# Attention with 32 groups of four heads: side work between the steps, tiles by twos, another engine for the maxima

## What is computed

```python
qkv = (x @ Wqkv + bqkv).reshape(B, L, 3, n_heads, head_dim)
scores = jnp.einsum('bqhd,bkhd->bhqk', q, k) / math.sqrt(head_dim)
scores = scores + slopes[None, :, None, None] * bias[None, None]
probs = jax.nn.softmax(scores, axis=-1)
out = jnp.einsum('bhqk,bkhd->bqhd', probs, v).reshape(B, L, D)
return out @ Wout + bout
```

## Time and profile before

| | us |
|---|---|
| median of three runs | 3262.87 |
| lowest, highest | 3258.28, 3268.13 |
| the profiled execution: its own time | 3271.27 |
| its span, first to last instruction | 3269.5 |
| attention, first to last exponential | 1250.1 to 2919.5 |
| PE busy over the span | 3085.7 (94%) |
| DVE, ACT, POOL busy | 2534.6, 1985.8, 1094.2 |
| mean granted TensorE clock | 0.952 of full speed |

### The profile page before, as it was taken

How to read it: one execution, slowest core, us unless ns; L and a number is a source line. 1 busy time by engine, 2 the same in 40 slices (tenths; PEclk the granted TensorE clock), 3 DMA queues, 4 the chain that set the end, 5 groups by cost and what they waited for, 6 DMA issues and landing times. The chain is left out here.

```text
span 3269.5 us, 73440 instructions
## 1 busy us (share of the span) xinstructions
PE 3085.7 (94%) x28196; PEld 1827.7 (56%) x28196; DVE 2534.6 (78%) x5875; ACT 1985.8 (61%) x2967; POOL 1094.2 (33%) x1364
## 2 busy tenths in 40 slices
PE   7999999995999869999999999999999999988999
PEld 3666666664788734444454444444544445437888
DVE  6677877764788658888888889788888887927887
ACT  2455444441666515777777777767777777775665
POOL 3354554443223221332423333323233232222222
PEclk8899999985999958999999999999999999998999
DMA  1000000002111151324232323232322322202111
GB/s 54 2 28 28 28 28 28 20 10 73 66 59 59 39 108 36 58 39 83 40 67 55 57 63 60 43 77 52 71 48 49 74 49 53 57 18 93 52 60 38
DMA packets 126461, 165.34 MB, mean 51 GB/s; under 512 B 23584, under 2 KB 104240, under 8 KB 125456
## 3 DMA queue, kind: packets, MB, share of 16 engines
q1 hardware_dynamic: 115688, 149.37, 18.7%
q0 software_dynamic: 9984, 10.38, 2.4%
q10 hardware_dynamic: 440, 0.90, 0.1%
HBM read 81.58 MB, written 38.24 MB: 37 GB/s over the span
## 5 line engine op out<-in xcount | busy, mean ns | idle before, releaser
L1855 ACT ACTIVATE b_p_t<-banks 128x1024 f32<-128x1024 f32 x1024 | 1040.2, 1027 | 304.0 <-PE banks L1742 238.7
L1681 PE MATMUL banks<-b_k_stack,b_q_stack 62*128 62x512 f32 x2048 | 809.6, 475 | 26.5 <-issue 10.8
L1742 PE MATMUL banks<-b_q_stack,b_k_stack 64*128 64x512 f32 x2048 | 767.8, 450 | 9.9 <-ACT b_p_t L1855 9.9
L1941 DVE CUSTOM_DVE_ANT_1 banks<-banks,b_near_rows 128x512 f32<-128x512 f32 x960 | 649.0, 715 | 138.3 <-PE banks L1681 135.1
L1944 DVE TENSOR_REDUCE b_half_max<-banks 128x1 f32<-128x512 f32 x1024 | 657.8, 684 | 79.9 <-PE banks L1681 76.3
L1696 PE MATMUL banks<-b_p_t,b_v 128*17 128x256 f32 x8192 | 631.8, 386 | 6.3 <-POOL b_p_t L2100 5.5
L1742 PEld LDWEIGHTS banks<-b_q_stack,b_k_stack 64*128 64x128 f32 x2048 | 313.7, 185 | 389.1 <-issue 325.5
L2100 POOL TENSOR_TENSOR b_p_t<-b_p_t,b_fall 128x256 f32<-128x256 f32 x384 | 280.5, 733 | 658.6 <-ACT b_p_t L1855 657.8
L1681 PEld LDWEIGHTS banks<-b_k_stack,b_q_stack 62*128 62x128 f32 x2048 | 341.9, 188 | 111.6 <-DVE b_half_max L1941 35.9
L1696 PEld LDWEIGHTS banks<-b_p_t,b_v 128*17 128x17 f32 x8192 | 142.8, 95 | 300.7 <-issue 162.2
L1148 ACT ACTIVATE ffn_relu<-banks,ffn_scale_fc 128x512 f32<-128x512 f32 x256 | 176.2, 688 | 205.5 <-PE banks L1080 205.5
(11 more groups left out here) (255 smaller groups left out, 5333.6 us busy)
## 6 DMA issues: line engine op xcount, KB each, us to landing
ffn_x<-x SPq DMA_DIRECT2D x32, 512.0 KB, 3.9
b_q_stack<-b_qk_hi SPq DMA_DIRECT2D x252, 64.0 KB
b_k_stack<-b_qk_hi SPq DMA_DIRECT2D x252, 64.0 KB
b_fall<-c_fall SPq DMA_DIRECT2D x48, 256.0 KB, 2.6
a_x<-hidden_states SPq DMA_DIRECT2D x16, 512.0 KB, 3.9
x<-a_x SPq DMA_DIRECT2D x16, 512.0 KB, 2.9
x<-ffn_x SPq DMA_DIRECT2D x16, 512.0 KB, 2.8
b_x<-x SPq DMA_DIRECT2D x8, 1024.0 KB, 5.6
```

Of the source, the lines that this page charges most:

```text
L1681: pe.matmul(m, q_stack[rows, slot, qb * P:(qb + 1) * P], k_stack[rows, slot, half * BANK:(half + 1) * BANK], start=True, stop=True, tile_p ...
L1742: last = pe.matmul(out, k_stack[stack, slot, kb * P:(kb + 1) * P], q_stack[stack, slot, half * BANK:(half + 1) * BANK], start=True, stop=n ...
L1855: act.activation(p_t[use % P_BUFS][:, :, :], scores[use % 2], ACT.Exp, scale=slopes()[pair][0]).then_inc(p_made, 1)
L1941: dve.tensor_tensor_reduce(out=m, in0=m, in1=near_window(pair, qb, rg), scale=1.0, scalar=LOWEST, op0=ALU.add, op1=ALU.max, accum_out=larg ...
```

## The change

- `attend` gives way once for each use instead of once for each score product (all five engines), and counts 32 steps: side work stands between uses.
- `make_stacks` counts 12 steps; the two projections are its steps 1 and 3, which fall ahead of use 4 and ahead of use 9. ACT evacuates each projection once (`qk`); POOL makes `qk_hi` from it by a copy and then `qk_lo`.
- SP issues the four transfers of bias rows (`stack_bias`) at step 1, before it waits for `qk_lo`; the 24 others follow the second projection as before, in the order of heads 0, 2, 1, 3, which is the order in which the maxima need them.
- Values and output tiles are made two at a time: twelve matmuls into one bank, one copy of 512 columns, one addition of 512 columns. `att_hi`, `att_lo` and `y` are now one buffer each of double width where there were two. Within a step of the output PE makes the product of the earlier two tiles before the transposes of the next two, and ACT copies in the same order.
- The maxima are transposed after the fourth of the next group's maxima (`turn == TURN - 1`, TURN is 4), and DVE copies the result out, ahead of its fifth maximum, instead of ACT. POOL's part, and SP's, stand at turn 5 instead of turn 3, one use later.

```diff
@@ schedule
-        STEPS, STACKS, VALUES, NORMALIZE = GROUP * HALVES * QB, 2, QB, 1 + QB
-        LEAD, TURN = 16, 2
+        STEPS, STACKS, VALUES, NORMALIZE = GROUP * HALVES * QB, 12, QB // 2, 1 + QB
+        STACK_STEPS = {1: 0, 3: 1}
+        LEAD, TURN = 16, 4
...
-                side_by_side(*([(STEPS, attend(g, rows), 1)] if g >= 0 else []),
+                side_by_side(*([(STEPS // ROWGROUPS, attend(g, rows), 1)] if g >= 0 else []),
...
-                             *([(STACKS, stacks(g + 2), 3)] if 0 <= g + 2 < ALL else []),
+                             *([(STACKS, stacks(g + 2), 1)] if 0 <= g + 2 < ALL else []),
...
+        IN_TURN = [pair + rg * PAIRS for pair in range(PAIRS) for rg in range(ROWGROUPS)]
@@ attend, on every engine
                     if rg == ROWGROUPS - 1:
                         follow(t, pair)
-                    yield
+                        yield
@@ tensor, find_maxima
-                    if g and turn == TURN:
-                        m, (used, n) = misc.take(("turn", g - 1), (shift_copied, g))
-                        pe.wait_ge(used, n)
-                        pe.wait_ge(row_max_made, g)
...
                         yield
+                    if g and turn == TURN - 1:
+                        m, (used, n) = misc.take(("turn", g - 1), (shift_copied, g))
+                        pe.wait_ge(used, n)
+                        pe.wait_ge(row_max_made, g)
...
+                    if g < ALL:
                         yield
@@ tensor, conclude
+                for n in range(TWOS + 1):
+                    tiles = TWOS * b + n
+                    if n:
+                        m, (used, value) = misc.take(("y", b, n - 1), (y_made, tiles))
+                        pe.wait_ge(used, value)
+                        pe.wait_ge(att_lo_made, tiles)
...
+                        last.then_inc(y_ready, 1)
+                    if n < TWOS:
+                        m, (used, value) = misc.take(("att", b, n), (att_lo_made, tiles + 1))
+                        pe.wait_ge(used, value)
...
                         last.then_inc(att_turned, 1)
@@ scalar, make_stacks
-                    act.activation(qk_hi[:, cols], m, ACT.Identity, bias=b_scaled[:, hg:hg + 1],
-                                   scale=scale_qk[:, 0:1]).then_inc(qk_hi_made, 1)
@@ scalar, find_maxima
-                        act.activation(shift_full[:, :], m, ACT.Copy, scale=-1.0).then_inc(shift_copied, 1)
@@ vector, find_maxima
+                    if g and turn == TURN:
+                        dve.wait_ge(max_turned, g)
+                        if g >= 2:
+                            dve.wait_ge(shift_made, g - 1)
+                        dve.tensor_scalar(shift_full[:, :], misc.at["turn", g - 1][0:2 * GROUP * QB, 0:P], -1.0, None, ALU.mult).then_inc(shift_copied, 1)
@@ gpsimd, make_stacks
-                    pool.wait_ge(qk_hi_made, use + 1)
...
+                        pool.tensor_copy(qk_hi[:, cols], qk[:, cols]).then_inc(qk_hi_made, 1)
+                        pool.wait_ge(qk_hi_made, use + 1)
+                        pool.tensor_tensor(qk_lo[:, cols], qk[:, cols], qk_hi[:, cols].bitcast(F32), ALU.subtract).then_inc(qk_lo_made, 1)
@@ sync, make_stacks
                 yield
-                yield
                 sp.wait_ge(bias_cast, 16)
+                if g >= SETS:
+                    sp.wait_ge(col_scores, STEPS * (g - SETS + 1))
+                for i in IN_TURN:
+                    stack_bias(sp, g, i)
+                for _ in range(max(STACK_STEPS) - 1):
+                    yield
                 sp.wait_ge(qk_hi_made, 2 * (g + 1))
                 sp.wait_ge(qk_lo_made, 2 * (g + 1))
-                if g >= SETS:
-                    sp.wait_ge(col_scores, STEPS * (g - SETS + 1))
-                for i in range(GROUP):
+                for i in IN_TURN:
                     if g or i < PAIRS:
                         stack_head(sp, g, i)
```

210 lines of the change are left out of this document (105 added, 105 removed).

## The result

The kernel after takes **3226.8 us** (median of 6 runs) where the kernel before, run beside it, takes 3260.6 (6 runs): a ratio of **0.9911, 95% interval 0.9883 to 0.9940**, some 29 us less (the two medians differ by 34). The profiled execution has 3227.1 us, its span is 3225.3, its mean granted clock 0.954 of full (before 0.952). Single executions of either kernel differ by 10 us and more, much of it in code that the change doesn't touch; attention began at 1126.0 us in this profile and at 1140.6 in the one of before. So what follows is read inside attention, which takes 1764.8 us from its first instruction to its last, where it took 1794.3: 29.5 less, which fits the ratio. Of that the loop (first to last exponential) has 33.7, the work ahead of it 2.6; the work behind it costs 6.8 more.

What follows compares the result with a forecast made beforehand. PE was taken to set the pace, with DVE as full in uses without side work. Terms of -50 us plus 4 for the clock took 3271.3 to 3225, and 3217 us on the median's scale; range 3188 to 3250.

Steps and rivals of the forecast that it cites:

- rival A: The forecast as worked out for the whole kernel: 3217 us, range 3196 to 3236; chance 0.60.
- Projections: Projections between uses with one ACT copy: 0.45 us saved at each of 53, -24 us.
- The first projection beside the statistics: Second groups of sequences 1 to 7: PE waits 3.0 us at use 3, +1.4 each, +10 us together.
- Maxima: Uses 24 to 26: copy on DVE costs 0.35 instead of the 1.50 lost, for 31 groups, -36 us.
- Values: Value tiles by twos: four pairs in seven groups at -0.25 us each, -7 us.
- Output in the loop: Output tiles by twos: nothing in the loop; last eight tiles some 16 us instead of 11.3, +4 us.
- POOL 0: Added rounding copy on POOL, 0.97 us each, covered before the product in use 7: 0 us.
- rival D: POOL's rounding copy holds back fallings, PE stops in use 7: slower, 3279 us at a 4.5 us copy; chance 0.06.
- The shift: Handover to next group: shift 0.2 us late in eight third groups, 1 us more after group 30; +3 us together.
- Clock: Lower granted clock after PE idles at the second groups' statistics: +4 us.
- rival C: Clock falls in all seven second groups (+23) and the shift comes late (+10): 3250 us; chance 0.12.
- Transfers: SP's 28 stack transfers reordered, bias rows first: no PE wait expected, 0 us.

Runs made afterwards that it cites:

- out_ones: Kernel after with output tiles one at a time again, two buffers each: last eight tiles 12.8 us (after: 18.1), first groups 0.5 us shorter.
- proj_3: Kernel after with each group's first projection ahead of use 3 instead of 4: uses 0 to 5 of second groups 11.03 us, loop 4.2 us shorter.
- copy_twice: Kernel after with the maxima copied twice by VectorE: uses 24 to 27 take 4.73 us (after: 4.72), loop 1635.9 us (after: 1635.6).
- val_ones: Kernel after with value tiles one at a time again: fourth groups 52.01 us (after: 51.1).
- early_shift: Kernel after with only POOL's split and SP's transfer of the shift back at turn 3: loop 12.6 us shorter.
- bias_back: Kernel after with the bias-row transfers issued behind the second projection again, each with its head: loop 2.3 us shorter.

## Why the prediction was right, and where not

The forecast of 3217 us lay 10 below the 3226.8 measured, inside its own range and on the right side; rival A is what happened. That the sum came so near is in part luck: the projections gave 12 more than forecast and the maxima 19 less, and 7.5 of the 29.5 us that attention gained stand in no term at all. In attention of the profiled executions the forecast has -46 and the profiles -29.5. Term by term:

- **Projections, -24 forecast.** Mechanism right, size too small: third and fourth groups and group 29 gained 1.25 to 1.4 us for two, first ones 0.9 (with the output counted off by `out_ones`), 0.4 to 0.7 each, and the second groups 1.3 in uses 5 to 10. All in all about -36. I had taken PE's 1.59 us as the floor; two projections in group 29 cost 1.38 each.
- **The first projection beside the statistics, +10.** Right in mechanism and place: PE stops at the second maximum of use 3, for 2.67 us (3.0 forecast), and uses 0 to 5 take 2.05 more: +14 (forecast +1.4 each, net of the gain). The lower clock has a share in that. Where the clock stays full, uses 0 to 5 take 10.41 us in the kernel before and in `proj_3`; at 0.70 behind the wait they take some 1.4 more in `proj_3`, and at 0.50 another 1.1 in the kernel after. By these rows I estimate that the clock costs some 12 us over the seven groups, against 5.7 before; so some 6 of the +14 are the clock and 8 the wait. `proj_3` shows that the place is the cause of both.
- **Maxima, -36 forecast.** This step failed. "DVE being full, all of that counts" charged the copy 0.35, and `copy_twice` shows a second one to cost nothing; and "1.50 - 0.35 = 1.15" took it that nothing else would be left of the 1.50, where 1.06 is left. Measured over uses 24 to 27: -0.45 in second and third groups, -0.6 in fourth ones (with the values counted off by `val_ones`), -0.8 in first ones, some -17 in all. What remains in use 25, two waits for a bank at DVE's pace and the transpose, I had not priced; what causes the two waits stays open.
- **Values, -7.** Right: 0.90 in seven groups, -6.3.
- **Output in the loop 0, tail +4.** The tail is +6.8; the chain that I had added up (3.7 us a pair) is the measured 3.66. I had 16 us for the whole against 18.1. Some 1.4 of the difference is the clock: the first pair runs at the lower one (matmuls 0.21 apart, later 0.12), and at full clock the same code takes 16.7. In the loop +0.5 for each of seven, inside the bounds.
- **POOL 0.** Its copy took 0.61 us, not 0.97, and rival D did not come in the kernel after: behind use 7 PE waits for POOL once, in group 1 (0.76), where it had waited before too. It came in `proj_3`, 1.08 us. But 0 was too little: late in the second groups PE waits 0.65 for POOL, where I had looked for nothing. These waits are counted with the shift below.
- **The shift, +3.** Right wait, too small: I had it short by 0.2 in eight groups (bound 0.8); it is 0.8 in third groups, 1.1 at the end of group 30, and 0.7 to 0.9 between uses 27 and 31 of second groups (against the kernel before, against `early_shift`), which I had let off; there PE waits for POOL and not for the transfer. `early_shift` returns 12.6 us. My way from the exponential to SP's issue was right (2.7 forecast, 2.62); the way from there to the product, "at most 4.0", I took from group 30, where it is 4.02 without a wait showing. In third groups it takes 4.7 to 5.1 where PE waits for it, and 3.9 was left.
- **Clock, +4.** Behind PE's stop of 2.67 us the granted clock fell in all seven second groups, to 0.50 to 0.70 over the next 5.7 us. Stops of 1.12 us in the kernel before and of 1.32 in `proj_3` brought it down in three of seven (0.72 to 0.86 over the 12 us from use 2 on). The Trainium skill (TensorE: Matmul & The Clock Gate, "HAM oscillation — how this bites in real kernels") has a loop whose bursts of matmuls are parted by longer waits for DMA, and in which every burst starts at the lower clock. Here the stops are shorter and stand in an otherwise full loop, and the longest of them had the same effect each time. So rival C's two mechanisms were both real: the handover at about C's price, the clock at half or less (some 1.4 to 2.5 us in a group against 5.0; it is counted in the +14 above). What kept the time below C's 3250 is what the projections gained.
- **Transfers, 0.** `bias_back` bears it out.

The table's terms (-36, +14, -17, -6, +3, +7, +13) make -22; the work ahead of the loop gives -2.6, which varies by more among kernels that don't touch it (106.3 to 110.4 us), and 5 us stay unassigned, 3 of them in uses 10 to 16 of the second groups.

What was to be seen came as written for the wait at use 3 and, better than written, for the projections (14.87 against 15.3); not for the maxima (3.38 against 2.8).

## What to carry to other kernels

An engine that is busy throughout doesn't make each of its operations count: the row maxima, ahead of the release of a bank that PE wants, seem to hold PE, and the copy, behind the transpose, doesn't. Double an operation and look at the pace-setter's next start, before charging it. When a step is moved, look at what each engine does at the new place: the shift's split landed behind a falling and the projection beside the statistics, and together these two places held back some 24 us, for edits of a few lines. Tiles by twos saved 0.9 us a group for the values, but for the output, with one buffer, they turned a chain that overlapped into one that doesn't, for 5.4 us at full clock. Compare such stretches at the same granted clock: 1.5 us between two variants was the clock alone.

## What the runs showed that I had not expected

- POOL's rounding copy of 128x512 takes 0.61 us, less than half of the 1.28 of the subtraction with two inputs of the same size; 256 columns with one input and two scalars take 0.55.
- VectorE, busy for 11.4 of the 12 us from 1993 to 2005 in the kernel after, took a second copy with no effect on the exponentials around it.
- The same output code takes 16.7 to 20.0 us from execution to execution, with the granted clock over it at 1.00 to 0.74. It is not only the single buffer, where PE stands 1.5 us in each pair: single tiles with two buffers take 11.3 to 13.7, at 1.00 to 0.75.
